# GpSimd makes the state input of 32 of 128 scan steps into the slot that the scan overwrites

## The reference

```python
def step(h, inp):
    x_t, d_t, B_t, C_t = inp
    dA = jnp.exp(d_t[:, :, None] * A)
    h = dA * h + d_t[:, :, None] * B_t[:, None, :] * x_t[:, :, None]
    y_t = jnp.sum(h * C_t[:, None, :], axis=-1)
    return (h, y_t)
```

## Time and profile before

| what | us |
|---|---|
| median of 3 runs | 733.44 |
| lowest and highest | 732.43, 739.20 |
| the profiled execution | 736.92 |
| its span, first to last instruction | 735.1 |
| first scan starts | 30.4 |
| scan loop ends | about 636 |

### The profile page before, as it was taken

One profiled execution on the slowest core, in us unless ns is written; L12 is line 12 of the kernel. 1 busy time (PEld: TensorE's weight loads), 2 busy tenths in 40 slices (PEclk: granted clock), 3 DMA queues, 4 the chain that ended last, 5 costly groups with the idle time before them and its releaser, 6 DMA issues. The chain is left out here.

```text
span 735.1 us, 9892 instructions
## 1 busy us (share of the span) xinstructions
PE 596.1 (81%) x3364; PEld 395.2 (54%) x3364; DVE 587.0 (80%) x592; ACT 495.3 (67%) x921; POOL 420.3 (57%) x234
## 2 busy tenths in 40 slices
PE   6686686888988969998698996898677677869995
PEld 2154363456554545545454554554444466659995
DVE  3599989998989759987697889788899899854442
ACT  3859834877598786897878789678966678313231
POOL 0078754555666464735566346675687567445663
PEclk9689879798999889999899997899899899989999
DMA  4670650075005700007400075003800751257771
GB/s 133 261 238 15 238 223 1 0 282 195 25 4 193 284 0 2 1 2 290 186 1 0 1 266 210 1 0 101 361 1 1 263 199 53 67 162 236 220 228 42
DMA packets 35661, 91.63 MB, mean 125 GB/s; under 512 B 7492, under 2 KB 13115, under 8 KB 35611
## 3 DMA queue, kind: packets, MB, share of 16 engines
q1 hardware_dynamic: 34138, 87.93, 34.1%
q0 software_dynamic: 1472, 3.06, 1.5%
HBM read 87.87 MB, written 3.11 MB: 124 GB/s over the span
## 5 line engine op out<-in xcount | busy, mean ns | idle before, releaser
L527 POOL TENSOR_TENSOR hc<-hst,bc 128x1024 f32<-128x1024 f32 x127 | 299.0, 2362 | 164.6 <-DVE hst L1096 78.8
L1108 DVE TENSOR_TENSOR_SCAN hst<-dA,bank 128x1024 f32<-128x1024 f32 x84 | 191.4, 2282 | 2.1 <-PE bank L1760 0.2
L671 ACT ACTIVATE dA<-delta,m_A_s 128x511 f32<-128x511 f32 x256 | 173.2, 712 | 9.1 <-DVE hst L1108 6.0
L1470 PE MATMUL bank<-ident,hc 128*128 128x128 f32 x1016 | 142.8, 289 | 12.8 <-POOL hc L527 12.7
L1470 PEld LDWEIGHTS bank<-ident,hc 128*128 128x128 f32 x1016 | 125.3, 151 | 42.9 <-issue 24.0
L1079 DVE TENSOR_TENSOR bank<-bank,bc 128x1024 f32<-128x1024 f32 x79 | 97.1, 1229 | 10.0 <-DMA bc<-crows 3.7
L1377 PE MATMUL bank<-arena 128*32 128x128 f32 (+6 forms) x466 | 52.6, 361 | 11.9 <-ACT arena L761 6.5
L467 POOL TENSOR_TENSOR du<-delta,xs 128x512 f32<-128x512 f32 x15 | 19.1, 1273 | 71.5 <-DVE delta L1120 71.5
L1096 DVE TENSOR_TENSOR_SCAN hst<-dA,bank 128x512 f32<-128x512 f32 x44 | 53.7, 1220 | 1.5
L1090 DVE TENSOR_TENSOR_SCAN hst<-dA,bank 128x512 f32<-128x512 f32 x44 | 53.5, 1215 | 0.8
L1377 PEld LDWEIGHTS bank<-arena 128*32 128x32 f32 (+3 forms) x466 | 26.5, 141 | 38.9 <-issue 21.5
(11 more groups left out here) (262 smaller groups left out, 1092.8 us busy)
## 6 DMA issues: line engine op xcount, KB each, us to landing
bc<-crows SPq DMA_DIRECT2D x126, 512.0 KB, 9.3
bc<-in_w SPq DMA_DIRECT2D x23, 512.0 KB, 4.0
xin<-in_xT SPq DMA_DIRECT2D x8, 256.0 KB, 4.4
rows_out<-arena SPq DMA_DIRECT2D x1, 1056.0 KB, 6.4
conv<-in_m_cw SPq DMA_DIRECT2D x2, 512.0 KB, 4.5
crows<-prow SPq DMA_DIRECT2D x8, 64.0 KB, 1.6
arena<-rows_out,source POOLq DMA_INDIRECT x23, 3.5
out_rows<-zs,target POOLq DMA_INDIRECT x23
```

The source lines that it names most:

```text
L527: pool.tensor_tensor(hc[:, g % HCRING], hst[:, g % HRING], bc[:, p, 1], ALU.mult) \
L671: act.activation(dA[:, g % RING, j, 1:], delta[:, h, 1:], ACT.Exp, scale=M[mamba_of(c)]["A"][:, h, n:n + 1]).then_inc(sems["dA"], 1)
L1108: dve.tensor_tensor_scan(hst[:, g % HRING].rearrange(flat), dA[:, g % RING].rearrange(flat), bank[:, first_bank:first_bank + 2, :].rearran ...
L1470: last = pe.matmul(bank[:, YB, P * j:P * j + P], hc[:, g % HCRING, n, P * j:P * j + P], ident[:], start=False, stop=s % PAIRS == PAIRS - 1 ...
```

## The change: what it does

For 32 steps (POOLED) DVE makes no product. POOL makes it, one 128x1024 instruction for both states, from du in SBUF and B, and writes it into the slot hst[g % 3] of the scan's ring. It is issued by drive_ahead right behind the C product of step g - 3 (POOL_LEAD), which was the last reader of the slot. The scan of the step then reads dA and this slot and writes the same slot in place; in the halved range 41 to 84 a pooled step thereby becomes one whole scan. The semaphore hc now counts both kinds of products on POOL, so every wait for it goes by hc_upto. All tables of half-steps hold new numbers; the instructions that they place stay the same.

```diff
+POOL_LEAD = 3
...
-NSTART = {1: 2, 2: 14, 3: 26}
-LATE_AT = 15
-Z_FIRST = (36, 39)
+NSTART = {1: 1, 2: 10, 3: 26}
+LATE_AT = 12
+Z_FIRST = (34, 37)
...
+POOLED = {0: ((), (3, 4)), 1: ((3, 5, 7), (1, 3, 5, 7)), 2: ((1, 2, 5), (1, 4, 6)), 3: ((7,), (1, 5, 6)), 4: ((2, 3),
+    (6, 7)), 5: ((4,), (3,)), 6: ((5, 7), (4, 6, 7)), 7: ((3, 7), ())}
...
         def dbu_upto(g):
-            return g - sum(1 for q in TURNED_STEPS if q < g)
+            return g - sum(1 for q in TURNED_STEPS + POOLED_STEPS if q < g)
+        def hc_upto(g):
+            return g + 1 + sum(1 for q in POOLED_STEPS if q - POOL_LEAD < g)
...
+            def drive_ahead(g):
+                c, s = g // STEPS, g % STEPS
+                h, p = s // PAIRS, s % PAIRS
+                pool.wait_ge(sems["du"], 2 * c + h)
+                if h == 0:
+                    pool.wait_ge(sems[BC_OF[p]], rows_in(c, p))
+                pool.wait_ge(sems["hc"], hc_upto(g - HRING))
+                pool.tensor_tensor(hst[:, g % HRING], du[:, h].unsqueeze(1).to_broadcast([P, 2, T]), bc[:, p, 0], ALU.mult) \
+                    .then_inc(sems["hc"], 1)
...
                             pool.tensor_tensor(hc[:, g % HCRING], hst[:, g % HRING], bc[:, p, 1], ALU.mult) \
                                 .then_inc(sems["hc"], 1)
+                        if g + POOL_LEAD in POOLED_STEPS:
+                            drive_ahead(g + POOL_LEAD)
...
             def halves_before(g):
-                return 2 * min(max(g - SINGLE[0], 0), len(SINGLE))
+                return 2 * sum(1 for q in SINGLE if q < g and q not in POOLED_STEPS)
...
-                if g in TURNED_STEPS:
+                if g in TURNED_STEPS or g in POOLED_STEPS:
                     return
...
             def scan(g):
+                if g in POOLED_STEPS:
+                    dve.wait_ge(sems["hc"], hc_upto(g - POOL_LEAD) + 1)
+                    dve.wait_ge(sems["dA"], 2 * g + 2)
+                    dve.tensor_tensor_scan(hst[:, g % HRING].rearrange(flat), dA[:, g % RING].rearrange(flat),
+                                           hst[:, g % HRING].rearrange(flat), 0.0, ALU.mult, ALU.add) \
+                        .then_inc(sems["scan"], 1)
+                    return
...
                     if g >= HRING:
-                        dve.wait_ge(sems["hc"], g - HRING + 1)
+                        dve.wait_ge(sems["hc"], hc_upto(g - HRING))
```

More of the change, by code:

```diff
@@ L37 @@
           (3, ((0,), (1,))), (3, ((2,), (3,))))
[L39 to L44, removed]
@@ new lines @@
+TAIL = (dict(ycp1=2, back1=3, gate1=3, out=4, res=5, ycp0=20, back0=30, gate0=31), dict(ycp1=4, back1=4, gate1=5,
+    out=6, res=6, ycp0=19, back0=31, gate0=32), dict(ycp1=5, back1=3, gate1=5, out=3, res=6, ycp0=19, back0=31,
+    gate0=31), dict(ycp1=2, back1=3, gate1=4, out=5, res=8, ycp0=19, back0=30, gate0=30), dict(ycp1=2, back1=3,
+    gate1=4, out=4, res=7, ycp0=19, back0=32, gate0=32), dict(ycp1=1, back1=3, gate1=5, out=5, res=12, ycp0=18,
+    back0=30, gate0=32), dict(ycp1=3, back1=4, gate1=7, out=5, res=8, ycp0=18, back0=30, gate0=34), dict(ycp1=3,
+    back1=8, gate1=17, out=8, res=27, ycp0=17, back0=27, gate0=50))
@@ L60 @@
 A0 = (8, 9, 8, 8)
 F0 = (11, 11, 11, 11)
[L62 to L66, removed]
+AAT = (dict(sq=0, var=0, rs=1, nrm=1, qk=4, qkc=3, v=4, vc=5, rec=29, rb=30, rbc=33, norm=32, o=33, h1=33), dict(sq=0,
+    var=0, rs=1, nrm=0, qk=2, qkc=5, v=5, vc=6, rec=30, rb=30, rbc=30, norm=32, o=32, h1=33), dict(sq=0, var=0, rs=0,
+    nrm=1, qk=3, qkc=2, v=3, vc=3, rec=28, rb=29, rbc=29, norm=31, o=31, h1=32), dict(sq=0, var=1, rs=2, nrm=1, qk=2,
+    qkc=2, v=2, vc=2, rec=32, rb=31, rbc=31, norm=34, o=34, h1=35))
@@ L77 @@
-NSTART = {1: 2, 2: 14, 3: 26}
-LATE_AT = 15
-Z_FIRST = (36, 39)
+FAT = (dict(sq=0, var=1, rs=3, nrm=3, gate=6, park=6, xh=3, visit=9, up=9, gu=11, down=14, x1=15, cen=15, cp=15,
+    st=18, rst=19, fc=20, fcp=20, gelu=26, hsq=26, hr=26, scale=26, turn=27, tc=27, proj=32, x2=34), dict(sq=0, var=3,
+    rs=3, nrm=3, gate=7, park=7, xh=7, visit=11, up=10, gu=11, down=16, x1=17, cen=17, cp=17, st=18, rst=18, fc=19,
+    fcp=19, gelu=22, hsq=24, hr=24, scale=25, turn=27, tc=28, proj=31, x2=34), dict(sq=0, var=2, rs=4, nrm=4, gate=5,
+    park=5, xh=6, visit=8, up=9, gu=10, down=15, x1=16, cen=16, cp=17, st=18, rst=18, fc=18, fcp=18, gelu=24, hsq=24,
+    hr=24, scale=27, turn=27, tc=27, proj=32, x2=33), dict(sq=1, var=0, rs=2, nrm=2, gate=2, park=4, xh=5, visit=8,
+    up=9, gu=9, down=15, x1=16, cen=16, cp=17, st=18, rst=18, fc=19, fcp=18, gelu=23, hsq=27, hr=27, scale=28,
+    turn=28, tc=29, proj=31, x2=36))
@@ L111, in build @@
     TURNED_STEPS = [STEPS * b + PAIRS * h + p for b in TURNED for h in range(HALVES) for p in TURNED[b][h]]
+    POOLED_STEPS = [STEPS * b + PAIRS * h + p for b in POOLED for h in range(HALVES) for p in POOLED[b][h]]
+    assert not set(POOLED_STEPS) & set(TURNED_STEPS) and all(g % STEPS for g in POOLED_STEPS)
     TURNED_HALVES = [(b, h) for b in TURNED for h in range(HALVES) if TURNED[b][h]]
@@ L1058, in halves_before @@
             def halves_before(g):
-                return 2 * min(max(g - SINGLE[0], 0), len(SINGLE))
+                return 2 * sum(1 for q in SINGLE if q < g and q not in POOLED_STEPS)
+            whole_again = min(q for q in range(SINGLE[-1] + 1, LAST) if q not in POOLED_STEPS)
             def drive(g):
@@ L1475, in accumulate_last @@
             def accumulate_last():
-                halved = 2 * len(SINGLE)
-                for n, blocks, made, count in ((1, range(QB), "half", halved + 1), (0, HALF_BLOCKS[0], "hc", LAST),
+                halved = 2 * len([q for q in SINGLE if q not in POOLED_STEPS])
+                for n, blocks, made, count in ((1, range(QB), "half", halved + 1), (0, HALF_BLOCKS[0], "hc", hc_upto(LAST - 1)),
                                                (0, HALF_BLOCKS[1], "half", halved + 2)):
```

51 lines of the change are left out of this document (22 added, 29 removed).

## The result

The changed kernel takes 773.67 us (median of 4 runs, 770.04 to 777.83) against 732.93 for the kernel before in the same job. The ratio, taken over all the runs and not from the two medians, is 1.053, 95% interval 1.0488 to 1.0572: 5% slower, outside the range of 711 to 746, on its slow side. Now and then an execution of any of these kernels falls into a slower state of the chip with a lower granted clock; all ratios here leave such executions out.

The account below looks back on a forecast made before the run. DVE bounds blocks 0, 1, 6, 7; DVE, PE and ACT wait for each other elsewhere. Block gains of 8.3 us less 4 for waits, tables 0, gave 736.9 - 4 = 733 us (729.5 on the median); 80% range 711 to 746.

Parts of the forecast that it names:

- DVE bounds blocks 0, 1, 6, 7; three engines share 2 to 5: Scan loop: DVE busy 94 to 96% in blocks 0, 1, 6, 7; in the others DVE, PE and ACT share the limit.
- rival A: Pooled scans don't hold the SBUF port: DVE's saving passes, 30 us less 5 for POOL, giving 708 us; chance 0.25.
- DVE loses 43 us of products: The 32 pooled steps: 20 whole save 1.229 us each, 12 halved save 1.546 each, 43 us of DVE time.
- The scan from SBUF has the same own price: Pooled scans reading two SBUF tiles: difference priced at 0, between -0.05 and +0.1 us each.
- POOL's product 2.362: POOL's 32 new products cost as much as the C product, 2.362 us each, 75.6 us in all.
- The port excludes a scan and a POOL product: A pooled scan and any POOL product exclude each other, so each pooled step takes 4.64 us of the port.
- What exclusion costs: Port demand summed per block against its length: gain 8.3 us with perfect packing, less 4 for waits, gain 4.
- all 32 waited half a product: Check on the pooled scans: 32 x 1.18 = 37.8 us of waits against 43 saved, gain 5.
- Who waits behind POOL: Behind POOL's new products stand the following C products, and for them PE's transposes and the ring of three; no price.
- Tables at 0, from -6 to +6: The remade tables of half-steps only move instructions between slots: taken as 0 us, bounds -6 to +6.
- Rival B: POOL and port become the bound: block 6 +10.8 us, block 1's second half +2.9, total about 745; chance 0.25.
- What would show it: Exclusion: scans' median 2.28 us, spread to 4.6. POOL-bound: block 6, block 1's second half each +5, blocks 3 to 5 not shrinking.

Follow-up runs that it names:

- the corners: Four kernels: POOL's product made or omitted, scan's second input SBUF (port) or PSUM; old tables, against kernel before: neither 0.9885, product 1.0067, port 1.023, both 1.0503.

## Why the prediction was wrong, point by point

- **DVE bounds blocks 0, 1, 6, 7; three engines share 2 to 5.** The busy shares were read rightly and the conclusion was too simple. Taking away the 43 us alone gave 10 us of loop where the prediction's rival A, before its 5 for POOL, gave 30. A busy share of 94% didn't mean that a piece taken out shortens the block. This step failed first. The prediction's words for it are "Then DVE's saving passes where DVE bounds" in rival A, and the forecast itself counted half of the savings in blocks 2 to 5.
- **DVE loses 43 us of products.** Right: L1102 is 59 products for 79, and 12 halved steps became whole.
- **The scan from SBUF has the same own price.** Right, 2.28 where nothing is in its way.
- **POOL's product 2.362.** Right: 2.371 without the port. The new wait on it cost DVE little directly (4.2 us before L1111 in all).
- **The port excludes a scan and a POOL product.** Right, and shown by the corners: 3.1 to 5.4%. This was the step on which the choice between forecast and A hung, and A is out on both counts.
- **What exclusion costs.** This is the step that failed most. I took the port as a resource whose demand is summed over a block and compared with the block's length, and gave a gain wherever there was room: "The port has room". The check beside it, that "all 32 waited half a product" on DVE alone, took the collisions as random and counted no price for POOL's side. The runs showed that 27 of 32 scans collide, most of them with a C product that the scan before released, and that both sides pay: 20 us in scans and some 44 of POOL. Blocks 3 to 5, with a gain of 8.5 us in the forecast, lost 15 when they alone were pooled, 1.3 of the 2.0% by the port. That the sum gave these blocks nine pooled steps and not ten changed it by 0.3 us. At step 91 a collision cost DVE 1.80 us for the 1.23 spared, so the saving was gone before any queue was counted.
- **Who waits behind POOL.** The prediction named PE's transposes and the ring of three, and gave them no price. They carried it: PE's wait for C products tripled (12.7 to 35.9 us), with attention and feed-forward behind it in PE's order, and PE's mean clock fell from 0.919 to 0.882.
- **Tables at 0, from -6 to +6.** Measured +9 alone, nothing together with the pooled steps. A small miss.
- **Rival B.** Its first place and price were right (block 6: 10.8 by the sum, 11.4 in the trace, 1.46% = 11 us by itself), and the corners fit its reason: with the tables of before, one trace each, the last 12 steps of the block take 49.4 us with neither product nor port, 49.5 with the port alone, 53.7 with the product alone and 57.6 with both (46.7 before). The second place was not: the second half of block 1 grew by 1.4 and not 2.9, the first half by 6.2. The total of 745 was 28 short, because it let the other blocks come out even.
- **What would show it.** The sign for exclusion came (scans from 2.28 to 4.44 with a median of 2.55, C products to 4.35); "over 10 us faster" didn't. The sign that I had set for B came only in part: block 6 grew by 11.4 and blocks 3 to 5 together didn't shrink (+5.6, +2.3, -0.8), but the second half of block 1 grew by 1.4 where 5 or more was asked. The loss is spread over more blocks than any of the three accounts had it.

No version of the pooled scan here beat the kernel before, down to four steps. With both the product and the port away these 32 steps gain about 1% (0.9885, and 0.993 with the new tables). A version whose decay lay in PSUM, leaving one SBUF input to the scan, wasn't tried.

## What to carry to other kernels

Before work is moved to POOL, ask which SBUF inputs the two engines then read at the same time, and which event releases each: two instructions that the same event releases collide again and again, however idle the engine is on average. Price such a move on both engines and on what stands in order behind the slower one. And measure what a saving is worth by leaving the work out on every engine first: here that one run would have said that 43 us of DVE were worth 8 to 10.

## What was not expected of the hardware

- A tensor_tensor_scan with both inputs in SBUF holds POOL's products off for all but the last 0.2 us of its 2.28, although it takes an element only every 2.2 ns. POOL instructions issued inside it showed up to 4.35 us for 2.36. By the corners a scan with one of its inputs in PSUM leaves POOL at 2.37.
- Between a C product and a scan the order of their starts decides to within 0.1 us: scan 29, issued 0.08 us after C(27), waited 2.14. But an instruction of POOL that itself waits can be passed. In the step 84 shown above POOL's scaling stands at 464.92, inside a copy of DVE (464.11 to 465.23); the scan is issued 0.23 us after it and still takes 2.28, and the scaling waits for both (the first of its four instructions takes 3.79 us for 1.56).
- Not every POOL instruction holds a scan for all of its length. In 11 cases a scan met the rest of a scaling instruction (1.56 us, one SBUF tile read): it waited 0.46 us where 1.47 were left, and nothing where 0.80 or less were. Why was not tested.
- Even an instruction of two elements in SBUF waits a POOL product out. In the run with four pooled steps (timeline, DVE and POOL) it took 1.76 us and ended with the C product beside it; in the run with the product and no port it took 0.17:

```profile
104.13 2.34 POOL L545 TENSOR_TENSOR hc<-hst,bc 128x1024 f32<-128x1024 f32 x1 [2.14 <-DVE hst L1137]
...
104.73 1.76 DVE L1053 TENSOR_SCALAR thr<-thr 128x2 f32<-128x2 f32 x1
```
